# One rolling order for a six-period transformer kernel, and a gated product moved off VectorE

## The reference

```python
x = x + tanh(g_xattn[0]) * performer(layernorm(x), ctx, ctx)            # 16 heads, 32 random features, causal
x = x + tanh(g_ffn[0]) * (self_attention + top-2 linear experts)(layernorm(x))
x = x + tanh(g_xattn[1]) * top64_attention(layernorm(x), ctx)           # 8 heads of 64 ("wide")
x = x + tanh(g_ffn[1]) * gated_experts(layernorm(x))                    # 8 experts, top 2, and a shared one
x = x + tanh(g_xattn[2]) * attention(layernorm(x), ctx, ctx)            # 16 heads
x = x + tanh(g_ffn[2]) * gelu_experts(layernorm(x))                     # 8 experts of 512, and a shared one
x = x + tanh(g_xattn[3]) * top32_attention(layernorm(x), ctx)           # 16 heads ("heads")
x = x + tanh(g_ffn[3]) * mixed_attention(layernorm(x))                # 16 experts mix q, k, v and the output
```

```python
h1 = permuted * m @ fc1_w[e]
proj, gate = jnp.split(h1, 2, axis=-1)
out_perm = out_perm + jax.nn.silu(proj) * gate @ fc2_w[e]
```

## Time and profile before

| | |
|---|---|
| median of 3 runs (lowest, highest) | 2301.85 us (2301.77, 2303.06) |
| the profiled execution | 2301.27 us |
| its span, first to last instruction | 2299.5 us |
| long block (six periods) in it | 381.2 to 1973.2, 1592.0 us |
| busy in the span: PE, DVE, ACT, POOL | 1966.4, 1950.7, 1469.7, 945.0 us |
| mean granted TensorE clock | 0.960 |

### The profile page before, as it was taken

How to read it: one execution, slowest core, us unless ns; L and a number is a source line. 1 busy time by engine, 2 the same in 40 slices (tenths; PEclk the granted TensorE clock), 3 DMA queues, 4 the chain that set the end, 5 groups by cost and what they waited for, 6 DMA issues and landing times. The chain is left out here.

```text
span 2299.5 us, 41471 instructions
## 1 busy us (share of the span) xinstructions
PE 1966.4 (86%) x12569; PEld 1561.2 (68%) x12569; DVE 1950.7 (85%) x7828; ACT 1469.7 (64%) x3637; POOL 945.0 (41%) x1374
## 2 busy tenths in 40 slices
PE   5778788889998899888998799888998889788677
PEld 4555567656976578656986579766886569667456
DVE  1289897989989898998989899898989989796982
ACT  3546477776777667776677667676577766477341
POOL 3232213544264434554165433554255542443441
PEclk9989999999999999999999999999999999899798
DMA  4000101000100101001100101001010001001000
GB/s 188 1 8 1 35 23 34 1 8 28 56 4 1 35 6 54 1 1 35 47 12 1 35 1 56 4 1 35 24 36 1 1 29 56 31 1 56 1 3 3
DMA packets 29503, 55.03 MB, mean 24 GB/s; under 512 B 2914, under 2 KB 10082, under 8 KB 28642
## 3 DMA queue, kind: packets, MB, share of 16 engines
q1 hardware_dynamic: 29282, 52.37, 7.0%
HBM read 51.31 MB, written 1.05 MB: 23 GB/s over the span
## 5 line engine op out<-in xcount | busy, mean ns | idle before, releaser
L265 DVE MATCH_REPLACE8 top_work<-top_eight,top_work 128x256 f32<-128x256 f32 x1664 | 667.9, 409 | 0.0
L267 DVE MAX8 top_eight<-top_work 128x8 f32<-128x256 f32 x1664 | 617.7, 413 | 0.2
L305 POOL TENSOR_TENSOR top_p<-top_p,top_rest 128x512 f32<-128x512 f32 x192 | 244.0, 1271 | 221.2 <-ACT top_rest L298 221.2
L850 PE MATMUL bank<-workP 128*128 128x256 f32 x1024 | 274.2, 392 | 38.4 <-ACT att_pP L990 31.8
L990 ACT ACTIVATE att_pP<-bank,att_tinyP 128x256 f32<-128x256 f32 x512 | 215.6, 479 | 65.7 <-DVE att_tinyP L1039 65.0
L850 PEld LDWEIGHTS bank<-workP 128*128 128x128 f32 x1024 | 177.9, 191 | 82.0 <-POOL workP L1012 34.9
L1039 DVE TENSOR_REDUCE att_tinyP<-bank 128x2 f32<-128x512 f32 x256 | 173.1, 680 | 20.1 <-PE bank L850 19.0
L645 PE MATMUL bank<-top_qk 128*128 128x256 f32 x512 | 146.1, 411 | 49.5 <-ACT top_p L286 41.9
L267 DVE MAX8 top_lead<-bank 128x8 f32<-128x256 f32 x384 | 144.8, 419 | 44.8 <-PE bank L645 23.5
L298 ACT ACTIVATE top_rest<-top_work,top_nmax 128x256 f32<-128x256 f32 x384 | 174.0, 507 | 10.3 <-DVE top_work L265 9.8
L286 ACT ACTIVATE top_p<-bank,top_nmax 128x256 f32<-128x256 f32 x384 | 159.6, 470 | 27.0 <-POOL top_nmax L273 18.0
(11 more groups left out here) (365 smaller groups left out, 4600.3 us busy)
## 6 DMA issues: line engine op xcount, KB each, us to landing
gelu_w<-in_pack3w SPq DMA_DIRECT2D x72, 256.0 KB, 3.0
top_qk<-in_pack3w SPq DMA_DIRECT2D x72, 256.0 KB, 2.8
pack<-in_pack SPq DMA_DIRECT2D x1, 4352.0 KB, 19.7
pack<-in_pack SPq DMA_DIRECT2D x1, 2266.0 KB, 9.8
pack<-in_pack SPq DMA_DIRECT2D x1, 1028.0 KB, 7.4
mix_wb<-in_ctx SPq DMA_DIRECT2D x1, 1024.0 KB, 4.8
x_in<-in_x SPq DMA_DIRECT2D x8, 128.0 KB, 2.1
ctx_tok<-in_ctx SPq DMA_DIRECT2D x8, 128.0 KB, 2.4
```

The costliest lines, as they stand in the source:

```text
L265: ins = nc.vector.match_replace(self.work[:, u % 2, j, :], eight, src, GONE)
L267: ins = nc.vector.max(eight, src)
L305: self.k.nc.gpsimd.tensor_tensor(v, v, self.rest[:, :, :], ALU.subtract).then_inc(*self.p_ready.one())
L850: mm = self.k.nc.tensor.matmul(self.banks[u % 2][:, j * T:(j + 1) * T], self.q1[:, u % self.RING, j * P:(j + 1) * P], self.kT, start=True, ...
```

## The change

The gated product is made without VectorE. The scalar engine takes the tanh first, into a tile of its own, and then copies both halves of the bank, proj and gate, to SBUF with the factor 0.5 (`halves`, a further 128x512 of a tile that is there). GpSimd makes (tanh + 1) * 2, multiplies it by half of proj, and then by half of gate. The bank is free for TensorE's next product as before, when the unit's product is made.

The two strings of a period become one, `ORDER` (543 letters), which `rolled` runs through again and again over three lanes that each hold the steps of all six periods. `SKIPPED` says how many letters of each lane the first pass leaves out, so that a lane begins at the letter from which its period counts, and ends there in the seventh pass. The lanes no longer meet in the middle of a period. For this the semaphores' counts are given beforehand (`k.sem(name, steps)`), and three waits are added which the fixed meeting had made needless. SyncE's loads and stores come in the order in which they came.

```diff
-ORDER_HEADS = (
-    "PPMQMPQQQQPQQPQQQPQQMQPPQQMMPPQQMMMPPQQQQPMQQQPQMPQQQQPMQQQPMQPQQQMMPPQPMMQQMMQQPPPQQQQPPMMQQQPPPPPPPMMPPPPQMP"
...
-ORDER_WIDE = (
...
+ORDER = (
+    "QPMQMPQPPQMMMQPQQQQPQPQPQPQPMQQPQPQQPQQQQQMQMPQQQQQQQPQQPMQPQQQQQPQQQQMPQQQPMMMPQQQMPQPQPQQQMQMQQPQQPPQPMMPQPQP"
...
+SKIPPED = {'Q': 69, 'P': 32, 'M': 19}
...
 class Signal:
-    def __init__(self, counter):
+    def __init__(self, counter, steps):
         self.counter, self.base = counter, counter.total
+        counter.total += steps
...
 class PlainHeads, dve:
         if s == 0:
+            if self.gated is not None:
+                dve.wait_ge(*self.gated.chain.done.at(1))
             yield from self.ln.dve_stats(dve)
...
 class WideStart, act and pool:
         if s == 0:
+            if self.wide is not None:
+                act.wait_ge(*self.wide.pv_done.at(H1))
...
 class GatedInOneBank:
-        self.th, self.hT = rest[:, 0, :], rest[:, 1:3, :]
+        self.th, self.hT, self.halves = rest[:, 0, :], rest[:, 1:3, :], rest[:, 6:8, :]
...
             act.wait_ge(*self.h_ps.at(u + 1))
-            nc.scalar.activation(self.hT[:, u % 2, :], self.bank[:, T:2 * T], ACT.Copy, scale=0.5).then_inc(*self.half_ready.one())
             if u >= 1:
                 act.wait_ge(*self.hT_ready.at(u))
             nc.scalar.activation(self.th, self.bank[:, 0:T], ACT.Tanh, scale=0.5).then_inc(*self.th_ready.one())
+            nc.scalar.activation(self.halves, self.bank[:, :].rearrange("p (c t) -> p c t", c=2), ACT.Copy,
+                                 scale=0.5).then_inc(*self.half_ready.one())
...
+            pool.wait_ge(*self.th_ready.at(u + 1))
+            nc.gpsimd.tensor_scalar(self.th, self.th, 1.0, 2.0, ALU.add, ALU.mult).then_inc(*self.u_ready.one())
             pool.wait_ge(*self.half_ready.at(u + 1))
-            pool.wait_ge(*self.u_ready.at(u + 1))
-            hT = self.hT[:, u % 2, :]
-            self.k.nc.gpsimd.tensor_tensor(hT, hT, self.th, ALU.mult).then_inc(*self.hT_ready.one())
+            pool.wait_ge(*self.u_ready.at(2 * u + 1))
+            nc.gpsimd.tensor_tensor(self.th, self.th, self.halves[:, 0, :], ALU.mult).then_inc(*self.u_ready.one())
+            pool.wait_ge(*self.u_ready.at(2 * u + 2))
+            nc.gpsimd.tensor_tensor(self.hT[:, u % 2, :], self.th, self.halves[:, 1, :], ALU.mult).then_inc(*self.hT_ready.one())
...
-            dve.wait_ge(*self.half_ready.at(u + 1))
-            dve.wait_ge(*self.th_ready.at(u + 1))
-            nc.vector.scalar_tensor_tensor(out=self.th, in0=self.th, scalar=1.0, in1=b[:, 0:T], op0=ALU.add,
-                                           op1=ALU.mult).then_inc(*self.u_ready.one())
...
+def rolled(lanes, order, skipped):
+    lanes, skipped, steps = {letter: iter(lane) for letter, lane in lanes.items()}, dict(skipped), []
+    while lanes:
+        for letter in order:
+            if skipped.get(letter, 0) > 0:
+                skipped[letter] -= 1
+            elif letter in lanes:
+                step = next(lanes[letter], None)
+                if step is None:
+                    del lanes[letter]
+                else:
+                    steps.append(step)
+    return steps
...
 flamingo, for i in range(2, NB):
-                run_steps(block, [heads, zero, first], ORDER_HEADS)
...
-                run_steps(block, [wide, rest, mix], ORDER_WIDE, loads)
+            lanes["Q"] += heads.steps() + wide.steps()
+            lanes["P"] += zero.steps() + rest.steps()
+            lanes["M"] += first.steps() + mix.steps()
...
+            run_steps(block, rolled(lanes, ORDER, SKIPPED), syncs)
```

More of the change, by code:

```diff
@@ L810, with __init__ @@
     RING = 4
[L812 removed]
+    def __init__(self, k, side, layer, x, ctxT, banks, tag, gate=None, router=None, before=None, start=None, gated=None):
         self.name = f"heads{layer}"
+        self.gated = gated
         self.k, self.x, self.banks, self.layer, self.gate = k, x, banks, layer, gate
@@ L2553, in run_block @@
 def run_block(k, chunks, order, loads=None):
+    around = [[loads.begin], [loads.finish]] if loads is not None else [[], []]
     with k.nc.Block() as block:
-        run_steps(block, chunks, order, loads)
+        run_steps(block, interleaved(chunks, order), around[0] + [c.sync for c in chunks] + around[1])
     k.end_block()
```

204 lines of the change are left out of this document (100 added, 104 removed).

## The result

The changed kernel takes 2285.91 us (median of 4 runs, 2280.85 to 2288.64) against 2301.81 us (4 runs, 2301.27 to 2303.06): a ratio of 0.9928, 95% interval 0.9910 to 0.9946. It is faster by 16 us, well over what a measurement tells. The forecast was 2253 us, a gain three times as large; its side was right, its size was not. The profiled execution took 2285.1 us, its span 2283.3, against 2301.27 and 2299.5.

A forecast was written before the change was run, and what follows sets the result against it. VectorE was taken to bound the heads half, TensorE nearly to fill the wide half. From 2301.85 us, -24.9 - 14.9 + 3.0 - 6.6 - 8.7 + 3.0 = -49.1 gave 2253 us, range 2223 to 2288, chance 0.53.

The forecast's parts named there:

- product off VectorE: Heads half: 60 products of 414 ns leave VectorE, -24.9 us, and its waits for the tanh, -14.9 (bounds 0 and 14.9).
- longer gated chain: Gated unit's longer chain counts only at the heads half's end: +0.5 us a period, +3.0 us (bounds 0 and 7.2).
- port lock: VectorE operations with two SBUF inputs stand still behind GpSimd's more often: +3.0 us (bounds 0 and 49).
- rival 3: GpSimd's in-order queue bounds the heads half, delaying line 305 or 1012 for TensorE: 2335 us; chance 0.07.
- the order: Steps exchanged nearby, mostly costed at nothing; gains only at the period's middle, -6.6 us, and end, -8.7 us.
- The heads half belongs to VectorE: In the half with the top-32 heads, VectorE is the bound: busy 121.61 of 134.30 us, TensorE 114.44.
- GpSimd's cover: Heads half: GpSimd's added 72.4 us are covered by idle time, 136.2 us of waiting for the removed VectorE products.
- The two places that I priced: Period's middle: first wide scores 1.1 us earlier, six times; period's end: chain to heads scores 1.74 us shorter, five times.
- Rival 1: Waits come back as VectorE waits for TensorE; only 24.9 us of busy time kept, +3.0 lock: 2280 us; chance 0.20.
- Rival 2: Gains more: last gated addition's 17.0 us wait goes, TensorE's clock stays up for 11.2 us: 2225 us; chance 0.14.
- Rival 4: Port lock catches a VectorE operation in each of 60 units, 49 us: 2299 us, no change; chance 0.06.
- The signs named ahead: Block about 1543 us, heads half 126 to 128, wide half 129 to 131, VectorE busy about 25 us less.

The follow-up runs named there:

- the GpSimd load held equal: Changed kernel without GpSimd's first two gated steps (tanh factor left out), read against the new order with the old product: 2256.16 us, ratio 0.9790 to the kernel before.
- the order alone: Rolling order with its waits and counted semaphores, gated product as in the kernel before: 2262.48 us, ratio 0.9800; once more 2257.34 us, 0.9795.
- the product first: Changed kernel with GpSimd's one product before its two other steps (tanh factor left out): 2269.94 us; with those two steps made twice: 2350.24 us.
- again: The changed kernel measured once more, unaltered, against the kernel before on the same chip: 2279.0 us, ratio 0.9890, block 1566.7 us.
- the cut order: Kernel before with the new order of steps inside each half, cut at the halves' ends so nothing rolls over: 2261.02 us, ratio 0.9809.
- the two waits of section 2: New order with the old product, plus two GpSimd waits keeping it off VectorE's closing addition and scalings at the period's end: 2252.35 us, ratio 0.9782.

## Why the forecast was right in its side and wrong in its size

By the terms of the sum, in us of block. The product's parts are read between kernels with the new order, the order's against the kernel before.

| term | forecast | measured |
|---|---|---|
| product off VectorE (busy, and its waits) | -24.9, -14.9 | -6.1 with the GpSimd load held equal, clock included |
| longer gated chain | +3.0 | +6 to +7 (1.1 a half) |
| port lock | +3.0 | none shown: 17 us of longer instructions in the block; 11 us of such tested, with the order alone, and off the path |
| GpSimd's load on its queue | 0 (rival 3) | about +17 (2.8 a half, read with the product first) |
| the order | -15.3 | -45.5 |
| clock, and what the parts do to each other | 0 | the rest, 3 to 7 |
| sum | -49.1 | -20.9 (again: -25.3); outside the block +4.7 |

- **What bounds the kernel.** "The heads half belongs to VectorE" was read from busy times, 121.6 of 134.3 us. It is the step that failed, and with it the largest term, -39.8 us. VectorE was the fullest engine, but with some 12 us of idle time it was no wall: with GpSimd's load held equal, freeing it of all its products brought 0 to 0.7 us a half. Part of the reason is that only 1.3 of 4.15 us of its busy time went; how much the longer operations hold back is open. What the runs show is a half in which several queues hand to each other: work put on VectorE (3.2 us for 2.4) or on GpSimd (10.3 for 2.8, then 10.2 for 10.6) costs, and work taken off VectorE did not pay by its length. That the wide half is TensorE's was right, and there was more in it: 131.2 us could become 127.5.
- **-24.9 - 14.9.** The count (60 of 414 ns) was right. The waits did not go with it: VectorE's idle time in the block went from 150 to 137 us with the order's help, and the wait of line 1798 grew to 22.0 (14.0 with the order alone, where VectorE's idle time is 99.7). The bound of 0 for the second term was nearer than the 14.9 that I took.
- **GpSimd's cover.** "Covered by GpSimd's idle time: it waited 136.2 us" took a sum of idle time for room. The idle time lay in front of each unit; the subtraction of line 305 comes when the top-p search is done, and finds the queue taken. Rival 3 named this mechanism and this line and had it at 0.07. It came in part: the two added steps cost 26.3 us of its 85, clock included. (Its threshold for a loss was mis-added: by its own sum 52 us are enough, not 55.) In the changed kernel itself most of TensorE's added wait stands before the product; that the same delay goes there through the subtraction is argued from the kernels with the product first, and not shown.
- **The chain.** +0.5 us a period, counted only at the half's end, was too little: it measures 1.1. TensorE meets the product within its queue in 31 units.
- **The port.** The kind was right: VectorE's operations are stretched behind GpSimd's. In the timeline of the changed kernel the two scalings on which the next heads scores hang began 0.06 us after line 305:

```profile
644.97 1.27 POOL L305 TENSOR_TENSOR top_p<-top_p,top_rest 128x512 f32<-128x512 f32 x1
...
645.03 1.54 DVE L358 TENSOR_SCALAR yP<-x,ln_mvP,ln_rstdP 128x128 f32<-128x128 f32 x2 [0.83 <-POOL ln_rstdP L363]
```

and in that of before they met nothing:

```profile
644.84 0.60 DVE L358 TENSOR_SCALAR yP<-x,ln_mvP,ln_rstdP 128x128 f32<-128x128 f32 x2 [0.83 <-POOL ln_rstdP L363]
```

The Trainium skill (SBUF — State Buffer, Who interferes with whom) lists tensor_scalar among the operations that can take the shared pair; with 1.54 us against 0.60 the trace agrees. That any of it is on the path is not shown, and where it was tested, it was not. The Trainium skill (Perfetto Trace Analysis, Optimizing Scalar/DVE Operations) says that offloading between VectorE and GpSimd might not help, because of the shared port. It did not help here, by 20.2 us behind the new order; but the cause that the runs show is GpSimd's added work, with the port's part not seen on the path where it was tested.
- **The order.** "Most of it I cost at nothing" was the other large miss, with the opposite sign, and the reason why the side was right. At the high clock it is 7.3 us a period where I had 2.55. The two places that I priced do move as I said: with the order alone VectorE's idle time before the heads maximum is 0.74 us, not 2.70, and the first wide scores come directly behind the heads products. Both places are in the cut order too, so their share of the 7.3 was not measured by itself. The waits say that it may be most: with the order alone VectorE's wait for the denominators (line 795, 18.8 us) is gone, that for the mixer's addition (6.8 us in the block) too, and that for the heads scores fell from 15.3 to 8.3. These 32.6 us stand against the 15.3 that I took; the upper bounds, 18.8 and 22.2, were nearer. A wait that goes is not yet time that goes, as the two waits of section 2 showed.
- **The rivals.** Rival 1 (2280 us) had the nearest number but the wrong reason: VectorE's idle time in the block is 136.9 us, not 165. Rival 2's clock went the other way. Rival 3 came in part, as said. Rival 4's 49 us did not come: VectorE's operations are 17 us longer in all.
- **The signs named ahead.** Block at 1543, heads half at 126 to 128: wrong. VectorE's busy time 25 us lower: wrong, 7.9. No wait over 2.27 us before GpSimd's first step: wrong, the longest is 4.1 (1.2 in the mean). VectorE's idle time before the first wide scores down by 1 us: it was 0.47 us and could not; it is 0.44, and what went is the wait of line 795 ahead of it. Wide half at 129 to 131: better than said. A heads half over 132 us was to overturn the forecast, and did.

What stays open: why the clock fell in some halves and not in others, which of the exchanged steps inside the halves carry the 7.3 us, and whether the longer VectorE operations hold back a kernel whose products have left VectorE.

## What to carry to other kernels

When two engines are each 90% busy and hand work to each other in order, neither busy time nor summed idle time is a price: ask where in the *receiving* engine's queue the added steps stand, who waits for them, and which late comer stands behind them. Measure a two-part change by its parts first; here one part gave 45 us of block and the other took 20 of them back (clock included), and the better kernel, the new order with the old product (2257 to 2262 us), was in between. Compare stretches of one kind at one granted clock, and look where in the stretch it fell: a half of 130 us often repeated to 0.1 us, where a median tells 0.2% of 2300.

## What the hardware showed that I had not expected

- GpSimd's operations stretch even small VectorE products: 16 columns, 1.17 us in place of 0.18 (line 1428) in every one of the periods. Which operation is struck changes with the order of steps and with the product: the same line on `rt_narrowM` took 1.2 us before, 0.18 with the order alone and 1.1 with the whole change.
- Eleven microseconds less of VectorE's busy time (the order alone with two waits more) left the halves at the high clock as they were and came back as 11.7 us of waiting.
- The price of one more GpSimd microsecond in a heads half rose from 0.27 (2.8 for 10.3) to 1.04 (10.6 for 10.2) between 71 and 92 us of load in a half of some 130.
- The same stretch of the same code ran at either clock in different periods of one execution, with 0.2 to 4.1 us of a half between them.
